# One-hot edge counting on Trainium2: loop bounds loaded as pairs behind each strip, in place of sixteen numbers ahead of each tile

## The reference

```python
dst = jnp.minimum((2500 * jax.random.uniform(key3, (80000,)) ** 2.0).astype(jnp.int32), 19999)
_o = jnp.argsort(dst, stable=True)      # edges come sorted by destination
src, dst = src[_o], dst[_o]
...
sums = jax.ops.segment_sum(x[src], dst, num_segments=2500)
# the kernel: A[src, dst] = number of edges src -> dst; sums = A^T x
```

## Time and profile before

| | us |
|---|---|
| median of 3 runs | 2962.51 |
| lowest and highest run | 2960.09, 2966.3 |
| the profiled execution | 2963.95 |
| its span in the trace | 2962.3 |
| the counting phase, first to last one-hot | 39.2 to 495.6 |

### The profile page before, as it was taken

One profiled execution on the slowest core, in us unless ns is written; L12 is line 12 of the kernel. 1 busy time (PEld: TensorE's weight loads), 2 busy tenths in 40 slices (PEclk: granted clock), 3 DMA queues, 4 the chain that ended last, 5 costly groups with the idle time before them and its releaser, 6 DMA issues. The chain is left out here.

```text
span 2962.3 us, 45354 instructions
## 1 busy us (share of the span) xinstructions
PE 2152.7 (73%) x12947; PEld 1641.3 (55%) x12948; DVE 1733.8 (59%) x4320; ACT 1109.1 (37%) x2240; POOL 565.5 (19%) x863
## 2 busy tenths in 40 slices
PE   5877886595593782583779349934988887579998
PEld 1233443353393441583349349932877776468887
DVE  7998886425347216666224755554778778345554
ACT  0234776101241101582124127722332232156665
POOL 2322332000302103473100147711000000001100
PEclk9788888697696895797899659966999999589999
DMA  1022343220000311464310035520222121000001
GB/s 43 36 89 106 145 174 160 97 107 1 29 1 4 144 40 45 136 184 132 143 65 1 20 125 168 168 88 19 86 76 86 52 77 36 12 23 11 21 22 35
DMA packets 133359, 222.56 MB, mean 75 GB/s; under 512 B 17565, under 2 KB 98973, under 8 KB 133075
## 3 DMA queue, kind: packets, MB, share of 16 engines
q1 hardware_dynamic: 122119, 190.51, 19.0%
q0 software_dynamic: 11088, 30.03, 3.3%
HBM read 146.27 MB, written 74.24 MB: 74 GB/s over the span
## 5 line engine op out<-in xcount | busy, mean ns | idle before, releaser
L2196 DVE SCALAR_TENSOR_TENSOR att_masked<-dinv_row,att_thr,x_feat 128x512 fp32r<-128x512 f32 x400 | 278.2, 749 | 109.2 <-PE att_ps L2308 94.1
L318 PE MATMUL count_ps<-hot_key,hot_lo 128*128 128x320 f16 x960 | 283.8, 358 | 49.5 <-DVE hot_key L300 28.4
L1917 DVE TENSOR_TENSOR e_h_low<-x_feat,e_h_high 128x512 fp32r<-128x512 f32 (+1 forms) x240 | 169.7, 709 | 245.2 <-ACT e_h_high L1842 245.2
L2308 PE MATMUL att_ps<-att_xl_parts,att_masked 128*128 128x260 f32 x1600 | 266.7, 313 | 59.3 <-DVE att_masked L2196 56.5
L299 DVE TENSOR_SCALAR hot_lo<-o_tok,key_stage 128x128 f16<-128x128 f16 x960 | 261.1, 272 | 49.1 <-POOL key_stage L281 45.3
L300 DVE TENSOR_SCALAR hot_key<-o_tok,key_stage 128x320 f16<-128x320 f16 x960 | 285.5, 297 | 0.2 <-issue 0.2
L797 PE MATMUL g_ps<-g_at,g_y 128*128 128x512 f16 x1170 | 261.4, 386 | 31.9 <-DMA g_at<-counts_t_high 26.3
L2308 PEld LDWEIGHTS att_ps<-att_xl_parts,att_masked 128*128 128x128 f32 x1600 | 222.2, 200 | 102.8 <-DVE att_masked L2196 76.1
L1841 ACT ACTIVATE x_feat<-e_hps,e_b 128x512 f32<-128x512 f32 (+1 forms) x240 | 177.7, 741 | 202.8 <-issue 99.8
L318 PEld LDWEIGHTS count_ps<-hot_key,hot_lo 128*128 128x128 f16 x960 | 98.1, 102 | 223.5 <-DVE hot_key L300 205.8
L797 PEld LDWEIGHTS g_ps<-g_at,g_y 128*128 128x128 f16 x1170 | 115.5, 99 | 175.2 <-DMA g_at<-counts_t_high 27.2
(11 more groups left out here) (471 smaller groups left out, 5211.9 us busy)
## 6 DMA issues: line engine op xcount, KB each, us to landing
g_at<-counts_t_high SPq DMA_DIRECT2D x12, 2560.0 KB
x_feat<-counts_high SPq DMA_DIRECT2D x40, 640.0 KB, 4.2
e_w_in<-in_L_ffn_W SPq DMA_DIRECT2D x35, 512.0 KB, 3.9
e_w_in<-in_L_ffn_expert_w SPq DMA_DIRECT2D x56, 256.0 KB, 3.3
counts_t_high<-turn_high SPq DMA_DIRECT2D x20, 640.0 KB, 3.0
counts_t_low<-turn_low SPq DMA_DIRECT2D x20, 640.0 KB, 4.2
counts_high<-row_high SPq DMA_DIRECT2D x20, 640.0 KB, 3.0
counts_low<-row_low SPq DMA_DIRECT2D x20, 640.0 KB, 4.1
```

Source lines behind the costliest of these rows:

```text
L318: pe.matmul(acc[:, q % 4, 0:KW], hot_lo[:, j, :], hot_key[:, j, :], start=False, stop=False, skip_group_check=True).then_inc(slot_free, 1)
L1917: dve.tensor_tensor(h_parts[i][1][:, v % 2, f, 0:w], h_sb[i][:, f, 0:w], h_parts[i][0][:, v % 2, f, 0:w].bitcast(F32), ALU.subtract).then_ ...
L2196: dve.scalar_tensor_tensor(S[:, n % RING, :], EL[:, it % 2, u - 1, :], thr[:, t, h:h + 1], A[:, t, :], ALU.is_gt, ALU.mult).then_inc(maske ...
L2308: mm = pe.matmul(ps[:, n % 2 * TB + q, 0:PW], side[:, q * P:(q + 1) * P], moving, start=(t == 0), stop=(t == NT - 1))
```

## The change

`ranges` becomes a tile of 21 x 8 x 2 numbers, with the two bounds of a strip side by side, and a 21st row of zeros. `bounds` loads the pair of one strip. Both engines load the 8 pairs of tile 0 ahead of the loop over tiles. Behind the loop of strip q in tile t, each loads the pair of strip q in tile t + 1 into the registers that this loop has just used. The load of 16 at the start of each tile is gone.

```diff
+            own.step(dve.memset(m.ranges[0:1, NT, :, :], 0))
...
-        def bounds(eng, t, regs):
-            eng.reg_load(regs, m.ranges[0:1, ds(t, 1), :].rearrange("a t n -> a (t n)"))
+        def bounds(eng, t, q, regs):
+            eng.reg_load(regs[2 * q:2 * q + 2], m.ranges[0:1, ds(t, 1), q, :].rearrange("a t n -> a (t n)"))
...
+            for q in range(QS):
+                bounds(pool, 0, q, regs)
             with pool.Fori(0, NT) as t:
-                bounds(pool, t, regs)
                 for q in range(QS):
...
-                    with pool.Fori(regs[q], regs[QS + q], UN) as c:
+                    with pool.Fori(regs[2 * q], regs[2 * q + 1], UN) as c:
...
                         pool.reg_add(used, used, 1)
+                    bounds(pool, t + 1, q, regs)
...
-                with pe.Fori(regs[q], regs[QS + q], UN):
+                with pe.Fori(regs[2 * q], regs[2 * q + 1], UN):
...
                     pe.reg_add(used, used, 1)
+                bounds(pe, t + 1, q, regs)
                 pe.matmul(acc[:, q % 4, 0:2], m.zeros16[:, :], m.src_no[:, 0:2], start=False, stop=False,
...
             def tile(t, u, before):
-                bounds(pe, t, regs)
                 for q in range(QS):
...
+            for q in range(QS):
+                bounds(pe, 0, q, regs)
             tile(0, 0, False)
...
-        m.ranges = sb("ranges", [1, NT, 2 * QS], I32)
+        m.ranges = sb("ranges", [1, NT + 1, QS, 2], I32)
```

More of the change, by code:

```diff
@@ L208, in _ @@
                                      ps[0:1, 3, :, 0:NH].rearrange("a (i u) t -> a i u t", i=2)))
-            own.join(dve.tensor_copy(m.ranges[0:1, :, :].rearrange("a t (i q) -> a i t q", i=2),
+            own.step(dve.memset(m.ranges[0:1, NT, :, :], 0))
+            own.join(dve.tensor_copy(m.ranges[0:1, 0:NT, :, :].rearrange("a t q i -> a i t q"),
                                      ends_row[0:1, :, :].rearrange("a i (t q) -> a i t q", q=QS)))
```

## The result

The kernel before takes 2961.61 us in the median (2960.09 to 2966.3), the changed one 3038.9 (3034.29 to 3041.82). The ratio is 1.0257, with an interval of 1.0239 to 1.0275: 2.6% slower, 77 us. The forecast was 2974.5 in a range of 2948 to 3000. The direction was right; the loss is six times the one forecast.

The account below looks back on a forecast made before the run. POOL's response time was taken to set DVE's pitch in the counting phase. 22.3 + 5.7 between strips, -21.8 at tile ends, +1.7 at the start and +4 for PE gave +11.9 us: 2974.5, range 2948 to 3000.

Parts of the forecast that it names:

- The price of a pair: Load of two numbers: 0.31 us on POOL, 0.36 on PE, at 0.053 per number; bounds 0.30 to 0.75.
- Under stores: Loads while the previous tile's stores are in flight: 16 numbers grow by 1.53 us, a pair by 0.19; 5.7 us in all.
- POOL's path between strips: POOL's step between stage writes grows from 0.79 to 1.09 us; 0.24 or 0.12 per load, 22.3 us quiet, 5.7 under stores.
- Rival 2: Between strips, POOL's idle time hides the pairs and the tile-end gains stay: -20 us, 2942; chance 0.15.
- POOL at a tile's end: Step across the end falls to 2.87 us from 3.62, or 5.13 under stores: 21.8 us gained over 14 and 5 ends.
- The start: Ahead of the loop, eight loads of 0.31 + 0.03 us replace one of 1.06: +1.7 us.
- PE: PE's pair loads are hidden at full clock; one turning strip in 12 tiles, at low clock under stores, costs 4 us.
- POOL's 1.755: DVE's pitch in us through POOL's path where every unit ends with a load, against 1.635 now.
- The sum: Whole kernel: 22.3 + 5.7 - 21.8 + 1.7 + 4 = +11.9 us, median forecast 2974.5.
- The memset of 16 numbers: DVE's memset at the start, with the other order of one copy, is worth 0.1 us or so, either way.
- rival 3: PE becomes the bound in all turning strips as its clock stays low: 22 us more than counted, 2997; chance 0.08.
- rival 4: Each pair load costs 0.556 us, as DVE's one load in this phase did: 30 us more, 3004; chance 0.07.

Follow-up runs that it names:

- load_sizes3: Kernel before plus loads of 1 to 16 zeros ahead of the first tile and of 1 and 2 in each tile, their numbers used: 3067.59 us, one run.
- pool_pairs_ps: Changed kernel with PE loading 16 numbers at each tile's start, POOL still loading pairs, the zero row's memset on POOL: 1.0193 to the kernel before.
- behind_poolset: Kernel before with POOL's load of 16 behind the move of keys, a tile ahead, zero row's memset on POOL, PE as before: 0.9961.
- pe_pairs_ps: Changed kernel with POOL loading 16 numbers at each tile's start, PE still loading pairs, the zero row's memset on POOL: 1.0225 to the kernel before.
- after_poolset: Changed kernel with the row of zeros written at the end of POOL's setup instead of on DVE: 1.0249 to the kernel before.
- after_warm: Changed kernel with three matmuls of zeros on PE ahead of each pair's load: 1.0229 to the kernel before.
- load_sizes: Kernel before with extra loads of several sizes ahead of the loop and two per tile, values unused: 3000.05 us against 3000.85 on that chip.

## Why the prediction was wrong, point by point

**The price of a pair: wrong, and the first step that failed.** "One to 16 numbers is 0.80 over 15, so 0.053 per number" joined two measured points with a line. Measured: 0.515 on POOL and 0.547 on PE. The bounds, 0.30 to 0.75, did hold it, and the one load that was nearest in kind, DVE's 0.556 in this phase, was set aside for 50 loads of one number. The Trainium skill's 600 ns for a tensor load, page "DMA: Bandwidth & Descriptors", section "Latency and other measured facts", lies closer to the pair than my line did. It is no floor here: one number takes 0.298 and four 0.324.

**Under stores: wrong.** I let the growth of 1.53 for 16 numbers go by the number, 0.19 for a pair. The times go as if by accesses, four of four numbers in a load of 16 and two of one in a pair, each growing by some 0.4 in the mean. The pair grows by 0.82 (0.515 to 1.33), four numbers by 0.46 (0.32 to 0.78). That sixteen grow by 1.53 fits four accesses, and `load_sizes3` bears it out with one number (0.6 at the worst, the pair 1.2). Counted as accesses, a pair costs half of what all sixteen numbers cost, and there are eight of them.

**POOL's path between strips: the step was right, the path a little high.** With a load of 0.515 it gives 0.20 + 0.515 + 0.58 = 1.30 for the step; measured is 1.26. With the measured sizes the same sum is 46 x 0.44 + 94 x 0.22 = 40.9 us quiet and 46 x 0.22 x 0.82 + 94 x 0.42 x 0.41 = 24.5 under stores: 65 where I had 28. `pool_pairs_ps` shows 73 (76 less 3), with PE's load of 16 under stores uncovered in it, which costs 16 in the first strips of `behind_poolset` and may cost more here, where it takes longer. So POOL's own part is below 60. Quiet strips show why: those of several units lose 0.34 where the sum has 0.44, single ones 0.14 to 0.19 where it has 0.22. Rival 2, that POOL's idle time hides the loads, is out; it hides 0.1 of one.

**POOL at a tile's end: right.** Forecast a gain of 21.8, measured 22 (60 to 38, seen from DVE). The 0.2 by which the step is longer than forecast (3.07 against 2.87) is the pair's 0.2; by POOL's steps alone it would have made the gain some 4 us less. Seen from DVE the quiet ends gain 0.84 each and not 0.75, those under stores 2.09 and not 2.26. That the sum agrees to 0.3 us is in part luck.

**The start: the working was right, the size wrong.** Eight loads of 0.51 with gaps in place of one of 1.06: 3.7 us, not 1.7.

**PE: wrong, and the largest miss.** I had 4 us, and `pe_pairs_ps` shows 68. Three things were in it. The pair's 0.547 takes the path over two strips from 3.45 to 3.64, 1.82 per strip, and at the clock of 0.73 in 468 to 474 the pitch is 1.90 to 1.93. "Just under POOL's 1.755" and "hidden, with nearly nothing to spare" were the warning; I priced what lay above that edge as if it could not be crossed. Under stores the forecast had 4.44 for two strips, with one slow load and the low clock in it. In `pe_pairs_ps` such a stretch takes 5.65 (417.21 to 422.86), with the load at 1.75, not 0.55. The growth of 0.97 by some 0.8 at 1.2 GHz had no row behind it: from the closing to the next products it is 1.37 there at that level (420.98 to 422.35), 0.4 more. And I counted one such strip in 12 tiles; in the changed kernel 38 of PE's loads lie under stores, one to three in each of the tiles 2 to 19. The strips 2 and 3 of a tile, counted from 0, alone carry 39.8 of the 70.8 us in `pe_pairs_ps`.

**The sum.** Forecast 28 for the strips by POOL, 4 by PE, -22 at the ends, 1.7 at the start. Measured +97, -22 and +3.7. Of the 97, 7 to 8 are the memset's (`after_poolset`), about 9 of the rest or somewhat more go with the clock (`after_warm`), and the others are the standing of POOL and PE during loads. How much of those is POOL's and how much PE's can't be given as a sum: alone they are worth 53.9 and 67.7 net, together 69.3.

**The memset of 16 numbers: wrong in kind.** "Worth 0.1 us or so" took its work for its price. Put into the kernel before it lengthens the phase by 20 us, 13 of them by DVE's delay. Nothing in the trace of before spoke of it.

**The rivals.** Rivals 3 and 4 were each true in their condition (PE the bound in turning strips; a pair near 0.556), and each had been priced alone, at 2997 and 3004. They come together, since both rest on the same load: 12 + 22 + 30 us would have been 3026.5. The range just held rival 3's figure and left out rival 4's, and neither together. Even 3026.5 is 12 short of the measured time.

## What to carry to other kernels

Splitting one load of registers into many small ones pays only if the small ones are cheap; read or measure the price at the very size, for it doesn't run in a straight line, and lay the numbers so that four neighbouring ones go in one load (here each starts at a multiple of four). An engine's sequencer stands during such a load, so it belongs where long work of that engine covers it (here behind the move of keys), and never between two instructions of a chain whose slack is some hundredths of a microsecond, on whichever engine. When two rivals rest on the same uncertain number, price them together before the range is set.

## What the runs showed of the hardware that was not expected

- A register load from SBUF takes 0.298, 0.515, 0.727, 0.324, 0.571 and 1.048 us for 1, 2, 3, 4, 8 and 16 neighbouring numbers on POOL. Two and three cost more than four.
- While stores keep the DMA share above 0.6, a pair takes 1.33 us in the mean and four numbers 0.78; sixteen take 2.6 at a share of 0.98. If accesses are counted as above, that is some 0.4 more for each. In `load_sizes3` the longest pair took 1.76 and the longest load of one number 0.92.
- One memset more on DVE ahead of its loop moved the delay from DVE's register row to the first instruction of a unit from 0.096 to 0.211 us at nearly all of the 240 units, and the whole kernel by 0.6%; two and eight, each followed by a wait, gave 0.103 and 0.096. The table's size by itself changed nothing (0.9992). A difference of this size between two kernels can come from an edit of the instructions ahead of a loop that costs 0.06 us itself.
- Register loads whose numbers nothing uses don't reach the program that runs: none of those added in `load_sizes` is in its trace.
